# Slot scores and running sum computed transposed, with projections and output products put in another order

## The chip, the core and the metric

One Trainium2 chip, one of its cores. The time is device microseconds for one execution of the whole program, the median of several; lower is better. Engines: PE is TensorE (matmuls), DVE is VectorE, ACT is ScalarE, POOL is GpSimd, SP issues most DMAs. Each runs its own instructions strictly in order and waits on semaphores for the others.

## What is computed

A gated slot attention layer and a scaled linear layer, each followed by a layer norm, for 4 sequences of 512 rows of 512 values, 16 heads. Cut to what matters:

```python
q, k = rope(hs @ Wq.T), rope(hs @ Wk.T); v = hs @ Wv.T; g = hs @ Wg.T
s = clip(hs @ Ws1.T @ Ws2.T + bs2, -32, 32)       # 64 slots for each head
es, enz = exp(s), exp(-cumlogsumexp(s, axis=time))  # enz = 1 / running sum of es
A  = where(mask, q @ k.T * DK ** -0.5, 0)
ok = enz * (A @ es)
qv = softmax(ok)                                   # over the 64 slots
W2 = where(mask, (qv * enz) @ es.T, 0)
o  = W2 @ v
o_n = o * rsqrt(mean(o * o) + EPS) * g_norm_weight
x = layernorm(hs + (o_n * silu(g)) @ Wo.T)
x = layernorm(x + x @ (weight * scale).T + bias)
```

## The kernel before

Four groups of four heads (g), inside each four sequences (b), inside each four chunks of 128 rows (c): 64 steps, written out in line by `all_steps_in_line`. A step i finishes the attention of chunk i and makes the projections, scores and exponentials of chunk n, the next one. Within a sequence two states are carried from chunk to chunk, `s1` (sum of k by es) and `s2` (sum of es by v); chunk 0 begins without them, chunk 3 updates none. Projections and the output product are split in a high and a low part, three products for each of four slices of the contraction: 12 matmuls of 512 columns (L842, called by `project`, or by the output loop into `bank_a`). The others are fp32 matmuls or transposes, which also run on TensorE (`transposes`, L856).

TensorE's order in a step: Q projection of n; `ok` of i (L960 from the masked scores, L962 from the state s1, four heads each, 64 columns wide); transposes of the normed and gated `o_gated` of the chunk before; K projection; transposes of q; slots of n (L982); V projection; transposes of the probabilities `slot_p`; output product of the chunk before into `bank_a`; W2 of i (L1010) and its part from s2 (L1015); transposes of es (n); running sum of es (`running_sum`, L869 to L872); G projection; transposes of k (n); o of i (L1038) out of the masked W2; updates of s1 and s2 (L1044, L1049); scores A of n (L879). A semaphore wait stands ahead of nearly each.

Behind o stands a chain on three engines, called the norm chain here: ScalarE squares o (L600), VectorE gates o (L803), sums the squares (L805) and makes `var` (L808), GpSimd takes `var` to the power -1/2 (L435, `rms`) and multiplies `o_gated` by it (L437). TensorE's transposes of `o_gated` in the next step wait for that. Behind `var` VectorE has in its queue `mask_a` (L673) and, in the step of chunk 0, the low part of the output weights `wo_lo` (L814). When a sequence is the group's last, the steps of chunks 2 and 3 also split the next group's weights: ScalarE makes the high parts (`w_split`, 128x2048), VectorE the low ones (L615); SP loads the next weight once the buffer of one is free.

`ok` is scaled by `enz` and its maximum taken on VectorE (L766, L769), shifted on GpSimd (L444), exponentiated on ScalarE (L567), summed on VectorE (L772) and multiplied by `enz` on GpSimd (L447). VectorE masks W2 at L678, and `enz` is a reciprocal of the running sum (L669).

Names in the trace that are views of others: `batch_raw` holds masked, o_sq, qT, kT, v and gate; `ws_raw` holds ok and slot_p; `small_ops` holds es, s1, s_clip and the constants; `bank_wo` holds W2, o, ok and slots.

Of the kernel before, what the change touches and what calls it, by code (L numbers as in the profile page):

```python
# [21 lines left out]
P = 128  # L22
# [3 lines left out]
HG = 4  # L26
# [20 lines left out]
for name, width in (("cos", CB * 64), ("sin", CB * 128), ("keep", P), ("below", P), ("identity", P), ("gnorm", 1),  # L47
                    ("ws2", HEADS * M)):
    start = sum(stop - first for first, stop in SMALL.values())
    SMALL[name] = (start, start + width)  # L50
# [3 lines left out]
def gated_slot_attention_block(nc, hs_cols, hs_rows, w_groups, ws1, small_in, ffn_w, ffn_scale, ffn_bias, out):  # L54
    with ExitStack() as ctx:
# [6 lines left out]
        def sem(name):  # L62
# [17 lines left out]
        cos_t, sin_t, keep, below_raw, ident, gn, ws2_raw = [small[:, a:b] for a, b in SMALL.values()]  # L80
        keep_r, below_r = sb("keep_r", P, F32R), sb("below_r", P, F32R)
# [10 lines left out]
        ok, slot_p = ws1_raw[:, 0:H], ws1_raw[:, H:2 * H]  # L92
        s1, s_clip, *es = [ws2_raw[:, H * k:H * k + H] for k in range(4)]
# [8 lines left out]
        esT = sb("esT", H)  # L102
        enz = sb("enz", H)
# [4 lines left out]
        pT, s2 = sb("pT", H), sb("s2", H)  # L108
# [5 lines left out]
        bank_qv, bank_kg, bank_t, bank_a, bank_c, bank_s2 = [  # L114
            bank(n) for n in ("bank_qv", "bank_kg", "bank_t", "bank_a", "bank_c", "bank_s2")]
        cums, s1_acc = bank_c[:, 0:H], bank_c[:, H:2 * H]
# [5 lines left out]
        slots_acc = bank_wo[:, H:2 * H]  # L122
        s2_acc = bank_s2[:, 0:H]
# [5 lines left out]
        def o_of(h):  # L129
            start = 512 * (h % 2) + H + P * (h // 2)  # L130
            return bank_wo[:, start:start + P]

# [16 lines left out]
        banks_T, banks_ffn = (bank_c, bank_s2, bank_a, bank_s), (bank_qv, bank_kg, bank_t, bank_o)  # L149
# [3 lines left out]
        for name in ("first", "second"):  # L153
# [15 lines left out]
        a_mm, ok_mm, w2_mm, o_mm, s1_mm, s2_mm, cums_mm = [  # L169
            sem(n) for n in ("a_mm", "ok_mm", "w2_mm", "o_mm", "s1_mm", "s2_mm", "cums_mm")]  # L170
        qT_mm, kT_mm, pT_mm, esT_mm, oT_mm = [sem(n) for n in ("qT_mm", "kT_mm", "pT_mm", "esT_mm", "oT_mm")]
        q_turned, q_summed, k_turned, k_summed = [sem(n) for n in ("q_turned", "q_summed", "k_turned", "k_summed")]
        qT_made, kT_made, v_made, s1_made, s2_made, a_masked, w2_masked = [
            sem(n) for n in ("qT_made", "kT_made", "v_made", "s1_made", "s2_made", "a_masked", "w2_masked")]
        th_made, gate_made, s_clipped, es_made, es_hi_made, es_lo_made, esT_made, enz_made = [
            sem(n) for n in ("th_made", "gate_made", "s_clipped", "es_made", "es_hi_made", "es_lo_made",
                             "esT_made", "enz_made")]
        ok_scaled, ok_maxed, ok_shifted, prob_made, prob_summed, slot_p_made, pT_made = [
            sem(n) for n in ("ok_scaled", "ok_maxed", "ok_shifted", "prob_made", "prob_summed", "slot_p_made",
                             "pT_made")]  # L180
# [203 lines left out]
        def _(pool):  # L384
# [47 lines left out]
            def step(u, g, b, c, last, left):  # L432
# [38 lines left out]
        def _(act):  # L471
# [32 lines left out]

            act.wait_ge(ones_set, 2)
# [6 lines left out]
            copy(keep_r[:, :], keep).then_inc(consts_made, 1)  # L512
            copy(below_r[:, :], below_raw).then_inc(consts_made, 1)
# [15 lines left out]
            from_bank(esT[:, :], bank_t[:, 0:H], esT_mm, 1, esT_made)  # L529
# [28 lines left out]
            def step(u, g, b, c, last, left):  # L558
# [8 lines left out]
                act.activation(ok[:, :], ok[:, :], ACT.Exp).then_inc(prob_made, 1)  # L567
# [45 lines left out]
        def _(dve):  # L613
# [144 lines left out]
            def step(u, g, b, c, last, left):  # L758
# [31 lines left out]
                if not left:  # L790
                    tick(2, 2)
# [343 lines left out]
```

## Time and profile before

| | before |
|---|---|
| median of 3 runs | 1510.54 us (1507.4 to 1511.48) |
| the profiled execution | 1510.89 us, of which 1509.1 us span |
| PE busy | 98% of the span, 9040 instructions |
| DVE busy | 58%, 876.1 us |
| POOL busy | 40%, 599.4 us |
| ACT busy | 35%, 529.3 us |
| mean granted clock of TensorE | 0.997 |
| chain that ended last | PE 96% |

The span runs from the first to the last instruction. The chain that ended last is followed back from the last instruction to whatever released each. A busy share of matmuls includes their pipeline, so what a block of matmuls costs is read here from the start of its first row to the start of the next block's first row.

### The profile page before, as it was taken

Reading aid. Unit: us, or ns where it says so; the run is one execution under the profiler, and the core shown is the slowest. Engines: PE = TensorE matmul, PEld = TensorE weight load, DVE = VectorE, ACT = ScalarE, POOL = GpSimd, SP = SyncE. Lnnn points to the kernel's source line nnn. Section 1 sums busy time; section 2 is a strip of 40 time slices with the busy share of each in tenths; the row PEclk is TensorE's granted clock in tenths of the full one; section 3 lists DMA queues with packets and bytes.
Section 4 is the critical chain, followed back from the end, with each engine's and each line's share of the span. In section 5 each row is a group of like instructions: output and inputs, shape, how many; then the busy total and the mean of one; then the engine's idle time right before and its main releaser. Section 6 shows DMA issues by size and latency. Waiting matters only on the chain.

```text
span 1509.1 us, 22779 instructions
## 1 busy us (share of the span) xinstructions
PE 1481.0 (98%) x9040; PEld 1236.9 (82%) x9040; DVE 876.1 (58%) x1488; ACT 529.3 (35%) x995; POOL 599.4 (40%) x573
## 2 busy tenths in 40 slices
PE   6999999999999999999999999999999999999988
PEld 3788888888888888888888888888888888888866
DVE  4555655556665556556755645555764555556567
ACT  5333323334332323333432323323432322323356
POOL 2424424443442344334434423433542343334345
PEclk9999999999999999999999999999999999999999
DMA  8211112022211202112420211112221111212223
GB/s 297 106 49 36 62 46 74 23 81 100 90 58 46 74 23 74 46 39 79 137 74 23 74 46 39 58 46 95 87 102 46 40 58 46 74 30 74 63 86 123
DMA packets 51414, 106.63 MB, mean 71 GB/s; under 512 B 5360, under 2 KB 15600, under 8 KB 46960
## 3 DMA queue, kind: packets, MB, share of 16 engines
q1 hardware_dynamic: 49008, 101.01, 20.2%
q10 hardware_dynamic: 2304, 4.20, 0.7%
q8 instruction: 72, 1.18, 0.3%
q14 instruction: 30, 0.25, 0.1%
HBM read 82.90 MB, written 22.28 MB: 70 GB/s over the span
## 4 chain that ended last, share of the span: by engine, by line
PE 96%; DVE 2%; DMA 1%; ACT 1%; issue 1%; POOL 0%; SPq 0%; POOLq 0%; DVEq 0%; ACTq 0%
PE bank_kg L842 24%; PE bank_qv L842 24%; PE bank_a L842 12%; PE bank_t L856 8%; PE bank_a L879 5%; PE bank_wo L1038 4%; PE bank_wo L960 3%; PE bank_wo L962 3%; PE bank_wo L1010 3%; PE bank_c L1044 3%; PE bank_s L1049 2%; PE bank_wo L1015 1%; DMA batch_raw<-hs_cols 1%; PE bank_c L869 1%; PE bank_wo L889 1%; PE bank_wo L842 1%
## 5 line engine op out<-in xcount | busy, mean ns | idle before, releaser
L435 POOL TENSOR_TENSOR rms<-var,minus_half 128x4 f32<-128x4 f32 x64 | 65.2, 1019 | 681.5 <-DVE var L808 681.5
L842 PE MATMUL bank_qv<-w_hi,hs_hi 128*128 128x512 f32 x512 | 207.4, 405 | 2.7 <-DVE w_lo L615 2.7
L842 PE MATMUL bank_kg<-w_hi,hs_hi 128*128 128x512 f32 x512 | 207.7, 406 | 1.0 <-DVE rope_b L635 1.0
L842 PE MATMUL bank_kg<-w_hi,hs_lo 128*128 128x512 f32 x512 | 202.3, 395 | 0.0
L842 PE MATMUL bank_qv<-w_hi,hs_lo 128*128 128x512 f32 x512 | 202.0, 395 | 0.0
L842 PE MATMUL bank_qv<-w_lo,hs_hi 128*128 128x512 f32 x512 | 201.8, 394 | 0.0
L842 PE MATMUL bank_kg<-w_lo,hs_hi 128*128 128x512 f32 x512 | 201.8, 394 | 0.0
L789 DVE TENSOR_TENSOR part<-bank_a,part 128x512 f32<-128x512 f32 x64 | 44.2, 691 | 231.8 <-PE bank_a L842 231.8
L473 ACT ACTIVATE oT_hi<-bank_t 128x512 fp32r<-128x512 f32 x65 | 38.9, 599 | 293.2 <-PE bank_t L856 293.2
L401 POOL TENSOR_TENSOR q_rot<-rope_a,rope_b 128x512 f32<-128x512 f32 x64 | 82.3, 1286 | 111.7 <-DVE rope_b L635 111.7
L669 DVE RECIPROCAL enz<-bank_c 128x256 f32<-128x256 f32 x64 | 112.3, 1755 | 9.7 <-PE bank_c L872 3.3
L842 PEld LDWEIGHTS bank_qv<-w_hi,hs_lo 128*128 128x128 f32 x512 | 95.8, 187 | 23.6
L842 PEld LDWEIGHTS bank_kg<-w_hi,hs_lo 128*128 128x128 f32 x512 | 95.8, 187 | 23.5
L842 PEld LDWEIGHTS bank_qv<-w_hi,hs_hi 128*128 128x128 f32 x512 | 96.4, 188 | 21.3 <-issue 3.5
L842 PEld LDWEIGHTS bank_kg<-w_hi,hs_hi 128*128 128x128 f32 x512 | 96.0, 187 | 19.2 <-issue 1.4
L842 PEld LDWEIGHTS bank_kg<-w_lo,hs_hi 128*128 128x128 f32 x512 | 96.2, 188 | 18.0 <-issue 0.2
L842 PEld LDWEIGHTS bank_qv<-w_lo,hs_hi 128*128 128x128 f32 x512 | 96.2, 188 | 17.7
L437 POOL TENSOR_TENSOR o_gated<-o_gated,rms 128x512 f32<-128x512 f32 x64 | 104.2, 1628 | 5.0
L842 PE MATMUL bank_a<-wo_hi,oT_hi 128*128 128x512 f32 x256 | 105.9, 414 | 0.0
L473 ACT ACTIVATE batch_raw<-bank_t 128x512 f32<-128x512 f32 x128 | 76.0, 594 | 78.9 <-PE bank_t L856 78.8
L664 DVE SCALAR_TENSOR_TENSOR batch_raw<-batch_raw,bank_kg 128x512 f32<-128x512 f32 x64 | 43.9, 686 | 101.3 <-ACT batch_raw L590 101.3
L842 PE MATMUL bank_a<-wo_hi,oT_lo 128*128 128x512 f32 x256 | 100.9, 394 | 0.0
(178 smaller groups left out, 3215.6 us busy)
## 6 DMA issues: line engine op xcount, KB each, us to landing
w_raw<-w_groups SPq DMA_DIRECT2D x32, 1024.0 KB, 5.0
x_scratch<-part SPq DMA_DIRECT2D x65, 256.0 KB, 2.0
hs_raw<-hs_cols SPq DMA_DIRECT2D x64, 256.0 KB, 2.8
part<-x_scratch SPq DMA_DIRECT2D x49, 256.0 KB, 2.9
batch_raw<-hs_cols SPq DMA_DIRECT2D x4, 1024.0 KB, 8.2
u_part<-u_scratch SPq DMA_DIRECT2D x64, 64.0 KB, 2.6
part<-hs_rows SPq DMA_DIRECT2D x16, 256.0 KB, 3.2
w_raw<-x_scratch SPq DMA_DIRECT2D x16, 256.0 KB, 2.7
```

What stands on the lines that cost most here:

```text
L401: pool.tensor_tensor(q_rot[:, :], rope_a[:, :], rope_b[:, :], ALU.add).then_inc(q_summed, 1)
L435: pool.tensor_tensor(rms[:, :], var[:, :], minus_half[:, :], ALU.pow).then_inc(rms_made, 1)
L437: pool.tensor_tensor(per_head(o_gated[:, :]), per_head(o_gated[:, :]), over_columns(rms[:, :], DV), ALU.mult).then_inc(o_norm_made, 1)
L473: return act.activation(dst, src, ACT.Copy, scale=scale)
L669: dve.reciprocal(enz[:, :], cums).then_inc(enz_made, 1)
L842: mm = pe.matmul(dst, x, y, start=start and n == 0, stop=stop and n == 2, **kw)
L856: mm = pe.transpose(bank_t[:, P * h:P * h + P], src[:, P * h:P * h + P], ident)
L879: mm = pe.matmul(bank_a[:, P * h:P * h + P], kT[:, P * h:P * h + P], qT[:, P * h:P * h + P], start=True, stop=True)
L960: mm = pe.matmul(dst, masked[:, P * h:P * h + P], es[now][:, slots], start=True, stop=c == 0)
L962: mm = pe.matmul(dst, qT[:, P * h:P * h + P], s1[:, slots], start=False, stop=True)
L1010: mm = pe.matmul(w2_of(h), esT[rows, at], pT[rows, at], start=True, stop=True)
L1038: mm = pe.matmul(o_of(h), masked[:, head], v[now][:, head], start=False, stop=True, skip_group_check=True)
```

## The change

- **`ok` is computed transposed.** es and s1 (64 columns) are now the stationary operand and the masked scores and qT (128 columns) the moving one; two heads go to the upper and lower 64 partitions of the same columns. VectorE scales it with the transposed reciprocal `enzT`, and two transposes on TensorE bring it back (`ok_acc`). VectorE then takes the maximum and does the shift, both from the accumulator; GpSimd's two operations on it are gone.
- **The running sum is fused with the transposes of es.** One product of es_hi/es_lo (stationary) with identity and keep mask side by side gives the transposed es and its transposed sum within the chunk; ScalarE copies both out and adds the last column of the chunk before as a bias. `below` is gone. `pT` is now multiplied by `enzT` on VectorE while it is copied out.
- **Order.** The output product follows the V projection directly. The probabilities' transposes, the fused sum and the G projection come next, then W2. The transposes of k and the updates of s1 and s2 stand ahead of o. s1 and s2 share an accumulator and are copied out by one instruction, ahead of the square of o.

```diff
@@ pool step @@
-                pool.wait_ge(ok_maxed, done(u, c))
-                pool.tensor_tensor(per_head(ok[:, :]), per_head(ok[:, :]), over_columns(ok_max[:, :], M),
-                                   ALU.subtract).then_inc(ok_shifted, 1)
-                pool.wait_ge(prob_made, done(u, c))
-                pool.tensor_tensor(slot_p[:, :], ok[:, :], enz[:, :], ALU.mult).then_inc(slot_p_made, 1)
@@ act @@
+            def turned(slot, n, first):
+                act.wait_ge(sumT_mm, n)
+                copy(two(esT[slot][:, :]), esT_acc).then_inc(esT_made, 1)
+                if first:
+                    copy(two(cumsT[slot][:, :]), cumsT_acc).then_inc(cumsT_made, 2)
+                else:
+                    for r in range(2):
+                        act.activation(cumsT[slot][:, P * r:P * r + P], cumsT_acc[:, r, :], ACT.Identity,
+                                       bias=cumsT[1 - slot][:, P * r + P - 1:P * r + P]).then_inc(cumsT_made, 1)
...
+                if c < CB - 1:
+                    from_bank(states[:, :], bank_c[:, :], states_mm, carried(u, c), states_made)
                 act.wait_ge(o_mm, i)
                 act.activation(by_parity(o_sq[:, :]), paired(1), ACT.Square).then_inc(o_squared, 1)
-                if c < CB - 1:
-                    from_bank(s1[:, :], s1_acc, s1_mm, carried(u, c), s1_made)
-                    from_bank(s2[:, :], s2_acc, s2_mm, carried(u, c), s2_made)
@@ dve step @@
+                dve.wait_ge(okT_mm, i)
+                dve.scalar_tensor_tensor(okT, okT_acc, SCALE, enzT[:, :], ALU.mult, ALU.mult).then_inc(ok_scaled, 1)
+                lo(oT_lo[:, :], bank_t[:, :], oT_hi[:, :], oT_hi_made, i, oT_lo_made)
                 dve.wait_ge(ok_mm, i)
...
+                dve.tensor_reduce(ok_max[:, :], per_head(ok_acc), AX.X, ALU.max).then_inc(ok_maxed, 1)
+                dve.wait_ge(ok_maxed, i)
+                dve.tensor_tensor(per_head(prob), per_head(ok_acc), over_columns(ok_max[:, :], M), ALU.subtract
+                                  ).then_inc(ok_shifted, 1)
                 if left:
                     rotate_k((c + 1) % CB, n)
                     clip(n)
...
+                dve.wait_ge(pT_mm, i)
+                dve.tensor_tensor(pT[:, :], bank_t[:, 0:H], enzT[:, :], ALU.mult).then_inc(pT_made, 1)
+                if left:
+                    dve.wait_ge(pT_made, i)
+                    make_enz((c + 1) % 2, n)
@@ pe @@
+            def turn_and_sum(slot, n):
...
+                for r in range(2):
+                    for x, half in enumerate((es_hi, es_lo)):
+                        mm = pe.matmul(bank_e[:, 2 * P * r:2 * P * r + 2 * P], half[slot][:, P * r:P * r + P],
+                                       ident_keep[:, :], start=x == 0, stop=x == 1)
+                mm.then_inc(sumT_mm, 1)
...
+                    mm = pe.matmul(okT_of(h), es[now][:, M * h:M * h + M], masked[:, head], start=h < 2,
+                                   stop=c == 0, skip_group_check=True)
...
+                        mm = pe.matmul(okT_of(h), s1[:, M * h:M * h + M], qT[:, head], start=False, stop=True,
+                                       skip_group_check=True)
...
+                pe.wait_ge(ok_scaled, i)
+                for r in range(2):
+                    mm = pe.transpose(ok_acc[:, P * r:P * r + P], okT[:, P * r:P * r + P], ident)
+                mm.then_inc(ok_mm, 1)
```

The order on TensorE, from the end of the output product to the first matmul of the G projection. Before:

```order
L842 MATMUL bank_a<-wo_hi,oT_lo 128x512
L1010 MATMUL bank_wo<-pT,esT 128x128 x4
L1015 MATMUL bank_wo<-s,pT 128x128 x4
L856 MATMUL bank_t<-small_ops 128x128 x2
L869 MATMUL bank_c<-es_hi,below_r 128x256
L869 MATMUL bank_c<-es_lo,below_r 128x256
L871 MATMUL bank_c<-es_hi,keep_r 128x256
L872 MATMUL bank_c<-es_lo,keep_r 128x256
L842 MATMUL bank_kg<-w_hi,hs_hi 128x512
```

After:

```order
L864 MATMUL bank_a<-wo_hi,oT_lo 128x512
L878 MATMUL bank_t<-small_ops,ws_raw 128x128 x2
L891 MATMUL bank_e<-ident_keep,es_hi 128x256
L891 MATMUL bank_e<-ident_keep,es_lo 128x256
L891 MATMUL bank_e<-ident_keep,es_hi 128x256
L891 MATMUL bank_e<-ident_keep,es_lo 128x256
L864 MATMUL bank_kg<-w_hi,hs_hi 128x512
```

W2 (L1010, L1015) has left this place, the transposes of es are gone, and those of the probabilities (`ws_raw`) have come from the other side of the output product.

The order on TensorE from the end of the G projection to the Q projection. Before:

```order
L842 MATMUL bank_kg<-w_hi,hs_lo 128x512
L856 MATMUL bank_t<-small_ops,k_rot 128x128 x4
L1038 MATMUL bank_wo<-batch_raw 128x128 x4
L1044 MATMUL bank_c<-small_ops,k_rot 128x64 x4
L1049 MATMUL bank_s<-batch_raw,small_ops 64x128 x4
L879 MATMUL bank_a<-batch_raw 128x128 x4
L842 MATMUL bank_qv<-w_hi,hs_hi 128x512
```

After:

```order
L864 MATMUL bank_kg<-w_hi,hs_lo 128x512
L1046 MATMUL bank_wo<-pT,esT 128x128 x4
L1050 MATMUL bank_wo<-states,pT 128x128 x4
L878 MATMUL bank_t<-small_ops,k_rot 128x128 x4
L1058 MATMUL bank_c<-small_ops,k_rot 128x64 x4
L1063 MATMUL bank_c<-batch_raw,small_ops 64x128 x4
L1073 MATMUL bank_wo<-batch_raw 128x128 x4
L899 MATMUL bank_a<-batch_raw 128x128 x4
L864 MATMUL bank_qv<-w_hi,hs_hi 128x512
```

W2 (now L1046, L1050) stands directly ahead of the transposes of k, and o (now L1073) comes behind the two state updates instead of ahead of them.

TensorE between the Q and the K projection: `ok`, then the transposes of `o_gated`. Before:

```order
L842 MATMUL bank_qv<-w_hi,hs_lo 128x512
L960 MATMUL bank_wo<-small_ops,batch_raw 128x64
L962 MATMUL bank_wo<-small_ops,batch_raw 128x64
L960 MATMUL bank_wo<-small_ops,batch_raw 128x64
L962 MATMUL bank_wo<-small_ops,batch_raw 128x64
L960 MATMUL bank_wo<-small_ops,batch_raw 128x64
L962 MATMUL bank_wo<-small_ops,batch_raw 128x64
L960 MATMUL bank_wo<-small_ops,batch_raw 128x64
L962 MATMUL bank_wo<-small_ops,batch_raw 128x64
L856 MATMUL bank_t<-small_ops,o_gated 128x128 x4
```

After:

```order
L864 MATMUL bank_qv<-w_hi,hs_lo 128x512
L978 MATMUL bank_wo<-batch_raw,small_ops 64x128 x4
L983 MATMUL bank_wo<-batch_raw,states 64x128 x4
L878 MATMUL bank_t<-small_ops,o_gated 128x128 x4
```

The eight alternating products 64 columns wide have become two groups with a 64-column stationary operand.

VectorE from the scaling of `ok` to the sum `eps_sum`, which goes into `var`. Before:

```order
L766 SCALAR_TENSOR_TENSOR ws_raw<-bank_wo,enz 128x256
L769 TENSOR_REDUCE ok_max<-ws_raw 128x4
L615 TENSOR_TENSOR oT_lo<-bank_t,oT_hi 128x512
L772 TENSOR_REDUCE p_sum<-ws_raw 128x4
L629 TENSOR_TENSOR rope_a<-bank_kg,small_ops 128x512
L635 TENSOR_TENSOR rope_b<-bank_kg,small_ops 128x4x64 x2
L659 TENSOR_SCALAR small_ops<-bank_wo 128x256
L778 SCALAR_TENSOR_TENSOR eps_sum<-p_sum 128x4
```

After:

```order
L783 SCALAR_TENSOR_TENSOR ws_raw<-bank_wo,enzT 128x256
L632 TENSOR_TENSOR oT_lo<-bank_t,oT_hi 128x512
L786 TENSOR_REDUCE ok_max<-bank_wo 128x4
L788 TENSOR_TENSOR ws_raw<-bank_wo,ok_max 128x256
L646 TENSOR_TENSOR rope_a<-bank_kg,small_ops 128x512
L652 TENSOR_TENSOR rope_b<-bank_kg,small_ops 128x4x64 x2
L676 TENSOR_SCALAR small_ops<-bank_wo 128x256
L794 TENSOR_REDUCE p_sum<-ws_raw 128x4
L796 SCALAR_TENSOR_TENSOR eps_sum<-p_sum 128x4
```

The maximum and the new shift stand behind the low part of oT, ahead of the rotation of k and the clip; the sum of the probabilities is behind the clip.

## Rows read from the trace of the kernel before

**Rows 1.** The page: the span, and TensorE's busy time and instructions.
```profile
span 1509.1 us, 22779 instructions
PE 1481.0 (98%) x9040; PEld 1236.9 (82%) x9040; DVE 876.1 (58%) x1488; ACT 529.3 (35%) x995; POOL 599.4 (40%) x573
```

**Rows 2.** Timeline of TensorE, 701 to 721 us: start, duration, engine, line, operation, count.
```profile
701.21 1.06 PE L1038 MATMUL bank_wo<-batch_raw 128*128 128x128 f32 x8
702.11 1.00 PE L1044 MATMUL bank_c<-small_ops,k_rot 128*128 128x64 f32 x8
703.04 0.66 PE L1049 MATMUL bank_s<-batch_raw,small_ops 128*64 128x128 f32 x8
703.63 1.16 PE L879 MATMUL bank_a<-batch_raw 128*128 128x128 f32 x8
704.54 0.48 PE L842 MATMUL bank_qv<-w_hi,hs_hi 128*128 128x512 f32 x1
...
707.42 0.33 PE L960 MATMUL bank_wo<-small_ops,batch_raw 128*128 128x64 f32 x2
...
709.15 0.61 PE L856 MATMUL bank_t<-small_ops,o_gated 128*128 128x128 f32 x4
...
712.41 0.60 PE L856 MATMUL bank_t<-small_ops,q_rot 128*128 128x128 f32 x4
...
712.97 0.39 PE L842 MATMUL bank_qv<-w_hi,hs_hi 128*128 128x512 f32 x1
...
715.77 0.38 PE L856 MATMUL bank_t<-small_ops,ws_raw 128*128 128x128 f32 x2
715.91 0.48 PE L842 MATMUL bank_a<-wo_hi,oT_hi 128*128 128x512 f32 x1
...
718.83 0.72 PE L1010 MATMUL bank_wo<-pT,esT 64*128 64x128 f32 x8
...
719.92 0.44 PE L856 MATMUL bank_t<-small_ops 128*128 128x128 f32 x2
720.12 0.36 PE L869 MATMUL bank_c<-es_hi,below_r 128*128 128x256 f32 x1
...
720.67 0.39 PE L842 MATMUL bank_kg<-w_hi,hs_hi 128*128 128x512 f32 x1
```

**Rows 3.** Timeline of GpSimd: the end of a norm chain, chunk 1.
```profile
705.65 1.04 POOL L437 TENSOR_TENSOR o_gated<-o_gated,rms 128x512 f32<-128x512 f32 x1
```

**Rows 4.** Timeline of TensorE, VectorE, GpSimd: the same chain behind chunk 0.
```profile
590.79 1.06 PE L1038 MATMUL bank_wo<-batch_raw 128*128 128x128 f32 x8
...
595.00 2.34 DVE L814 SCALAR_TENSOR_TENSOR wo_lo<-w_raw,small_ops,wo_hi 128x2048 fp32r<-128x2048 f32 x1
...
595.24 3.01 POOL L437 TENSOR_TENSOR o_gated<-o_gated,rms 128x512 f32<-128x512 f32 x1
```

**Rows 5.** Timeline of GpSimd and TensorE: the one time that TensorE waited for it.
```profile
1410.40 2.46 POOL L437 TENSOR_TENSOR o_gated<-o_gated,rms 128x512 f32<-128x512 f32 x1
...
1412.91 0.66 PE L856 MATMUL bank_t<-small_ops,o_gated 128*128 128x128 f32 x4 [0.29 <-POOL o_gated L437]
```

**Rows 6.** Timeline of VectorE: the mask of W2.
```profile
720.04 0.69 DVE L678 TENSOR_TENSOR batch_raw<-bank_wo,small_ops 128x512 f32<-128x512 f32 x1 [0.41 <-PE bank_wo L1015]
```

**Rows 7.** Timeline of VectorE, GpSimd, ScalarE: a step in which weights are split.
```profile
712.61 0.69 DVE L629 TENSOR_TENSOR rope_a<-bank_kg,small_ops 128x512 f32<-128x512 f32 x1 [0.78 <-PE bank_kg L842]
...
715.27 2.28 DVE L615 TENSOR_TENSOR w_lo<-w_raw,w_hi 128x2048 fp32r<-128x2048 f32 x1
...
715.29 2.86 POOL L409 TENSOR_TENSOR es_lo<-small_ops,es_hi 128x256 fp32r<-128x256 f32 x1
...
722.84 1.91 ACT L473 ACTIVATE w_hi<-w_raw 128x2048 fp32r<-128x2048 f32 x1 [2.05 <-DMA w_raw<-w_groups]
```

**Rows 8.** Timeline of GpSimd and VectorE: the end of that step.
```profile
727.86 1.02 POOL L435 TENSOR_TENSOR rms<-var,minus_half 128x4 f32<-128x4 f32 x1 [9.71 <-DVE var L808]
...
728.24 2.28 DVE L615 TENSOR_TENSOR w_lo<-w_raw,w_hi 128x2048 fp32r<-128x2048 f32 x1
```

More of the change, by code:

```diff
@@ L46 @@
 SMALL = {}
-for name, width in (("cos", CB * 64), ("sin", CB * 128), ("keep", P), ("below", P), ("identity", P), ("gnorm", 1),
+for name, width in (("cos", CB * 64), ("sin", CB * 128), ("keep", P), ("identity", P), ("gnorm", 1),
                     ("ws2", HEADS * M)):
@@ L131, in o_of, with okT_of @@
             return bank_wo[:, start:start + P]
+        def okT_of(h):
+            rows, at = slice(64 * (h % 2), 64 * (h % 2) + 64), H + P * (h // 2)
+            return bank_wo[rows, at:at + P]
         def paired(bank_half):
@@ L696, in _ @@
             clip(1)
-            make_enz(1)
+            make_enz(0, 1)
             make_gate(0, 1)
@@ L1002, in step @@
                 mm.then_inc(out_mm, 1)
+                pe.wait_ge(prob_made, i)
+                if left:
+                    pe.wait_ge(qT_made, n)
+                transposes(prob, HG // 2).then_inc(pT_mm, 1)
+                if left:
+                    pe.wait_ge(cumsT_made, 2 * i)
+                    turn_and_sum(nxt, n)
+                    pe.wait_ge(k_turned, n)
+                    if last and c == CB - 1:
+                        w_ready(g * 4 + 8)
+                    project(WG, bank_kg, nxt).then_inc(g_mm, 1)
+                if not left:
+                    tick(1, 1)
                 pe.wait_ge(pT_made, i)
+                pe.wait_ge(esT_made, i)
                 if left:
@@ L1009, in step @@
                     rows, at = slice(64 * (h % 2), 64 * (h % 2) + 64), slice(P * (h // 2), P * (h // 2) + P)
-                    mm = pe.matmul(w2_of(h), esT[rows, at], pT[rows, at], start=True, stop=True)
+                    mm = pe.matmul(w2_of(h), esT[now][rows, at], pT[rows, at], start=True, stop=True)
                 if c:
-                    pe.wait_ge(s2_made, carried(u, c - 1))
                     for h in range(HG):
@@ L1018, in step @@
                 if left:
-                    pe.wait_ge(es_made, n)
-                    transposes(es[nxt], HG // 2).then_inc(esT_mm, 1)
-                    running_sum(nxt, n, c == CB - 1)
-                    pe.wait_ge(k_turned, n)
-                    if last and c == CB - 1:
-                        w_ready(g * 4 + 8)
-                    project(WG, bank_kg, nxt).then_inc(g_mm, 1)
                     pe.wait_ge(k_summed, n)
-                    pe.wait_ge(esT_made, n)
                     transposes(k_rot[nxt]).then_inc(kT_mm, 1)
+                if c < CB - 1:
+                    for h in range(HG):
+                        pe.matmul(s1_acc[:, M * h:M * h + M], k_rot[now][:, P * h:P * h + P],
+                                  es[now][:, M * h:M * h + M], start=c == 0 and h == 0, stop=True,
+                                  skip_group_check=True)
+                    for h in range(HG):
+                        rows, at = slice(64 * (h % 2), 64 * (h % 2) + 64), slice(DV * (h // 2), DV * (h // 2) + DV)
+                        mm = pe.matmul(s2_acc[rows, at], es[now][:, M * h:M * h + M], v[now][:, DV * h:DV * h + DV],
+                                       start=False, stop=True, skip_group_check=True)
+                    mm.then_inc(states_mm, 1)
                 if not left:
-                    tick(1, 1)
                     pe.wait_ge(part_made, i)
@@ L1112 @@
         "keep": keep_mask,
-        "below": 1 - keep_mask,
         "identity": np.eye(P, dtype=np.float32),
```

124 lines of the change are left out of this document (47 added, 77 removed).

## The prediction

> **What bounds the kernel now.** I read the page first: TensorE is busy for 1481.0 of 1509.1 us [rows 1], and the list of waits gives it only a handful in the whole program. So the kernel costs what TensorE's blocks cost, and a change pays by shortening blocks as long as no other engine becomes late. Then the timeline of TensorE over one step: since durations overlap, I take a block from its start to the next one's start [rows 2]. Then, on the timelines of the other engines, what each of TensorE's semaphores would be late by once blocks are shorter or moved. The profiled execution took 1510.89 us, within 0.4 us of the median of the runs (1510.54); the sum is made against 1510.9.
>
> **TensorE's own work.** From [rows 2], per step:
> - `ok` now takes 707.42 to 709.15, 1.73 us for eight products, each 64 columns on a 128-column stationary operand. Afterwards it is eight products with 64 stationary columns, two heads side by side. The update of s2 is that form: four in 703.04 to 703.63, 0.59 us, with going into and out of the half-width layout. The nearest row for eight in one go is W2 with its s2 part, 718.83 to 719.92, 1.09 us, though that halves rows, not columns. The bounds are 0.87 (a pure doubling of the part without the transition, an estimate) and 1.18 (twice 0.59). I take 1.04: 0.69 less. In chunk 0, which has only four: about 0.87 to 0.59, 0.28 less.
> - Two transposes bring `ok` back: +0.21, by the two of es (719.92 to 720.12). The two of es go: -0.20.
> - The output product takes 715.91 to 718.83, 2.92; behind a projection and not behind transposes it costs what V costs, 712.97 to 715.77, 2.80: -0.12. In that 2.92 was 0.04 for the half-array form behind it (Q, which also follows fp32 work, takes 704.54 to 707.42, 2.88); that now falls on G, +0.04, and Q gets another 0.04 for `ok`.
> - The sum keeps four products of 256 columns (720.12 to 720.67, 0.55), but a sequence's first chunk had only two: +0.28 in the step of chunk 3.
>
> Steps of chunks 1 and 2: -0.69 + 0.21 - 0.20 - 0.12 + 0.04 + 0.04 = -0.72 each; chunk 3: -0.44; chunk 0: -0.31. Four make -2.19 us, sixteen sequences -35.0 us. Were that all, the time would be 1476.
>
> **Waits that appear.** Four are ended by rows, and they eat it.
>
> First, the norm chain behind chunk 0. From the start of o at 590.79 GpSimd's multiplication ends at 595.24 + 3.01 = 598.25, 7.46 us later [rows 4]. Behind other chunks it takes 705.65 + 1.04 - 701.21 = 5.48 [rows 2, 3]: GpSimd gets nowhere while VectorE makes `wo_lo`. TensorE used to have s1, s2, the scores, Q and `ok` to do meanwhile, and now s1 and s2 (702.11 to 703.63, 1.52 us) lie ahead of o. It arrives after o 0.90, scores 0.91, Q 2.92 and `ok` 1.04: 5.77 us. In return the mask of A no longer waits for scores that stood behind s1 and s2. It follows `var` directly, and so `wo_lo` starts about 0.4 after the start of `rms`, as the split in [rows 8] does (728.24 against 727.86), and not about 0.86 after it (595.00 against 594.14, which is 595.24 less 1.10) [rows 4]. That brings the chain's end to 6.98, and TensorE started 0.05 behind it the one time it waited (1410.40 + 2.46 to 1412.91) [rows 5]. The wait is 7.03 - 5.77 = 1.26 us, 16 times: 20.2 us. How long `ok` takes doesn't matter here; chain and wait together are fixed.
>
> Second, the same chain behind chunk 3: 5.48 + 0.05 = 5.53 against 0.90 + 0.91 + 2.92 + 0.59 = 5.32, so 0.21, 16 times: 3.4 us. Behind chunks 1 and 2 it is 5.53 against 5.77, no wait, 0.24 of slack.
>
> Third, the mask of W2. It starts 0.12 behind the start of the block after W2 (720.04 against 719.92) and takes 0.69 [rows 2, 6]; with 0.1 for the signal back (an estimate, twice the 0.05 above) o may start 0.91 behind W2's end. G used to cover this. Now the transposes of k do (0.43) and s1 and s2 (1.52); the step of chunk 3 has no updates, and there 0.48 is left, 16 times: 7.7 us. VectorE's other new work ahead of that mask (copy of pT 0.42, reciprocal 1.75 by the groups of the profile) starts with the output product and the fused sum and ends inside G, 2.84 us long; in chunk 0, where ScalarE makes `wo_hi` before it copies the sums, about 0.7 us of cover is left.
>
> Fourth, the group's last sequence. The rotation of k stands behind the maximum and the shift now. It used to start 0.20 behind the transposes of q (712.61 against 712.41). Now it comes after those transposes 0.35, the signal 0.46, the maximum 0.46 and the shift 0.36, 1.63, so 1.43 later [rows 2, 7]. In ordinary steps the fused sum, though it is earlier than the old one by W2, still finds `es_lo` more than a microsecond early. Where VectorE splits weights, GpSimd's `es_lo` is held up by it: 2.86 us long, ending at 718.15, 2.88 behind the start of the split at 715.27 [rows 7]. Shifted by 1.43 it ends 7.17 behind the start of the transposes of q, and the sum is due after 0.35 + 0.21 + 0.20 + 2.80 + 2.80 + 0.14 = 6.50: 0.7 us, in two steps of three sequences. In the first of the two, the high part of the next V weights waits for their load, which waits for that split. It started 5.29 behind the split's end (722.84 against 717.55). Shifted, it ends so late that the copies of kT and the square of o stand behind it: about 0.3 for the scores, and 1.3 for the norm chain, which meets a split as chunk 0's does. Sum 0.7 + 0.7 + 0.3 + 1.3 = 3.0, three times: 9.0 us. The last sequence of all, with the split of the linear layer's weights in the same places, I put at 1.4.
>
> Waits: 20.2 + 3.4 + 7.7 + 9.0 + 1.4 = 41.7. 1510.9 - 35.0 + 41.7 = **1517.6 us**. GpSimd loses 1.35 us of work a step (L444, L447), which pays nothing, as it isn't what is late. VectorE gains about 0.8 us a step at 58% busy. SP's queue is not reordered; its loads of weights come later with the splits, which is in the fourth wait. The new bias copies on ScalarE (two for one, some 0.3 each) end inside G.
>
> **Two rules of the skill.** GpSimd's 3.01 us beside 1.04 and its end 1 us behind VectorE's operation show that one shuts the other out [rows 3, 4]. The Trainium skill, SBUF — State Buffer, section "Who interferes with whom", says that the port pair these engines share goes whole to whichever starts first, a VectorE operation with two SBUF inputs or a GpSimd one that reads SBUF. By that `wo_lo`, once it starts inside `rms`, would itself wait for the end of `rms`. The row speaks against it: the split starts 0.38 into a `rms` and lasts 2.28 [rows 8], no longer than the one that starts just ahead of GpSimd's work [rows 7]. It is a rival below. The Trainium skill, TensorEngine Tiling, section "Key Properties", says that a change of tiling mode drains the engine. The change adds two such changes a step; the 0.04 and the part of 0.59 above are what the rows give for it.
>
> **The rivals.**
> - The covers hold: the mask of W2 and the splits come in time, because VectorE runs a little ahead of my sum. Without the third and the fourth wait it is 1517.6 - 7.7 - 9.0 = 1501, faster. For it: these are sums of half a microsecond built from many terms. Against: W2's mask is one operation behind one block, and short of terms. Chance 0.14. It decides where both vanish; where one of them does, the time is 1508.6 to 1509.9, no difference: 0.25, with a half-width `ok` at its lower bound (32 steps by 0.17, 5 us) among it.
> - The norm chain is not late behind chunk 0 either, and the change pays in full: 1476. That needs GpSimd to multiply beside `wo_lo`, and every chunk 0 shows 3.01 us. Chance 0.04.
> - `rms` shuts out `wo_lo` once they overlap: it starts 0.64 later (1.02 - 0.38), the chain ends so much later behind 16 chunks 0 and three splits: 19 x 0.64 = 12.2, 1530. Chance 0.10.
>
> **How the numbers follow.** The forecast's own case, some 1515 to 1526, has 0.47. About 0.3% (4.5 us) is what a measurement of this kernel can tell from no change. Slower is the forecast and the shut-out, 0.57; same 0.25; faster 0.14 + 0.04 = 0.18. The range from 1501 to 1530 leaves out the full gain and the tails.
>
> **What would show it.** The changed kernel's waits should list TensorE waiting for `o_gated` of GpSimd some 35 times, with about 1.2 us the common long one; for the mask of W2 some 15 times with 0.5; for `es_lo` six times. The `ok` block should take 1.0 to 1.1. A step of chunk 1 should be 0.5 us longer than before, one of chunk 2 0.7 shorter. If the waits for GpSimd are missing, the norm chain was misread; if `ok` takes over 1.2, the tiling was.

## The result

| | before | after |
|---|---|---|
| median of four runs (lowest to highest), us | 1510.18 (1507.4 to 1511.48) | 1524.88 (1523.71 to 1527.88) |
| profiled execution and its span, us | 1510.89, 1509.1 | 1524.71, 1522.9 |

The changed kernel takes 1.0099 times as long, with a 95% interval of 1.0086 to 1.0113: 14.7 us slower. The forecast was 1517.6, slower by 7; the sign and the range held, the size was half of what came. Between the two profiled executions it is 13.8 us.

The page of the changed kernel, its head and the chain that ended last by engine:

```profile
span 1522.9 us, 22779 instructions
...
PE 1459.8 (96%) x9072; PEld 1187.4 (78%) x9072; DVE 895.2 (59%) x1616; ACT 525.0 (34%) x995; POOL 502.5 (33%) x445
...
PE 79%; POOL 8%; DVE 5%; ACT 4%; issue 3%; DMA 1%; POOLq 0%; SPq 0%; DVEq 0%; ACTq 0%
```

TensorE is busy for 21 us less than in [rows 1], and the program is 14 us longer. GpSimd, with 97 us less to do, now holds 8% of the chain that ended last. The list of waits says where (who waited <- for whom: us in total, times, longest):

```profile
PE bank_t L878 <- POOL o_gated L446: 28.3, 36, 1.4
...
PE bank_e L891 <- POOL es_lo L418: 3.8, 6, 0.6
PE bank_wo L1073 <- DVE batch_raw L695: 3.1, 15, 0.2
```

The three kinds of wait that were forecast are all there, and as often as forecast: some 35 for `o_gated`, some 15 for the mask of W2, six for `es_lo`. On TensorE's timeline the 36 for `o_gated` are 16 of 1.24 us behind the chunks 0, 15 of 0.20 behind the chunks 3, three of 1.18 in the last sequences of groups (1.3 forecast) and two of 1.43 and 0.59 in the final sequence. The common long one, behind chunk 0, on the timelines of TensorE, GpSimd and VectorE of the changed kernel (start, duration, engine, line, operation, count; in brackets the idle time before and who ended it), which answers to [rows 4]:

```profile
684.32 1.16 PE L1073 MATMUL bank_wo<-batch_raw 128*128 128x128 f32 x8
685.32 1.06 PE L899 MATMUL bank_a<-batch_raw 128*128 128x128 f32 x8
686.13 0.48 PE L864 MATMUL bank_qv<-w_hi,hs_hi 128*128 128x512 f32 x1
...
689.11 0.66 PE L978 MATMUL bank_wo<-batch_raw,small_ops 128*64 128x128 f32 x8
...
691.44 0.66 PE L878 MATMUL bank_t<-small_ops,o_gated 128*128 128x128 f32 x4 [1.23 <-POOL o_gated L446]
```
```profile
687.77 1.02 POOL L444 TENSOR_TENSOR rms<-var,minus_half 128x4 f32<-128x4 f32 x1 [10.83 <-DVE var L830]
688.87 2.51 POOL L446 TENSOR_TENSOR o_gated<-o_gated,rms 128x512 f32<-128x512 f32 x1
```
```profile
688.15 2.34 DVE L836 SCALAR_TENSOR_TENSOR wo_lo<-w_raw,small_ops,wo_hi 128x2048 fp32r<-128x2048 f32 x1
```

o starts at 684.32, GpSimd ends at 688.87 + 2.51 = 691.38, and TensorE goes on at 691.44. So the chain with its signal takes 7.12 us; 7.03 was forecast. TensorE's own work beside it ends 1.2 us before.

An ordinary step, timeline of TensorE, which answers to [rows 2]; blocks are again taken from start to start:

```profile
704.63 0.71 PE L1046 MATMUL bank_wo<-pT,esT 64*128 64x128 f32 x7
...
705.72 0.66 PE L878 MATMUL bank_t<-small_ops,k_rot 128*128 128x128 f32 x4
706.21 1.00 PE L1058 MATMUL bank_c<-small_ops,k_rot 128*128 128x64 f32 x8
707.14 0.66 PE L1063 MATMUL bank_c<-batch_raw,small_ops 128*64 128x128 f32 x8
707.73 1.16 PE L1073 MATMUL bank_wo<-batch_raw 128*128 128x128 f32 x8
708.73 1.06 PE L899 MATMUL bank_a<-batch_raw 128*128 128x128 f32 x8
709.54 0.48 PE L864 MATMUL bank_qv<-w_hi,hs_hi 128*128 128x512 f32 x1
...
712.52 0.66 PE L978 MATMUL bank_wo<-batch_raw,small_ops 128*64 128x128 f32 x8
713.01 0.61 PE L983 MATMUL bank_wo<-batch_raw,states 128*64 128x128 f32 x8
713.54 0.66 PE L878 MATMUL bank_t<-small_ops,o_gated 128*128 128x128 f32 x4
713.95 0.48 PE L864 MATMUL bank_kg<-w_hi,hs_hi 128*128 128x512 f32 x1
...
716.84 0.60 PE L878 MATMUL bank_t<-small_ops,q_rot 128*128 128x128 f32 x4
717.27 0.38 PE L1004 MATMUL bank_wo<-small_ops,ws_raw 128*128 128x128 f32 x2
717.41 0.37 PE L1008 MATMUL bank_wo<-ws_part,u_part 128*128 128x256 f32 x1
717.61 0.39 PE L864 MATMUL bank_qv<-w_hi,hs_hi 128*128 128x512 f32 x1
```

| block, us | before | forecast | after |
|---|---|---|---|
| Q | 2.88 | 2.92 | 709.54 to 712.52, 2.98 |
| `ok` | 1.73 | 1.04 | 712.52 to 713.54, 1.02 |
| transposes of `o_gated` | 0.37 | 0.37 | 713.54 to 713.95, 0.41 |
| transposes of q, and of `ok` | 0.35 | 0.35 + 0.21 | 716.84 to 717.41, 0.57 |
| output product | 2.92 | 2.80 | 2.74 |
| fused sum, with the transposes of es before | 0.75 | 0.55 | 0.57 |
| G | 2.80 | 2.84 | 2.87 |
| transposes of k | 0.43 | 0.43 | 705.72 to 706.21, 0.49 |
| o and the scores together | 1.81 | 1.81 | 1.00 + 0.81 |

And the steps, from the start of one o to the start of the next (ordinary sequences; a step repeats within 0.02 from sequence to sequence, but for one of 21.07 in the place of 20.95):

| step from the o of chunk | 0 | 1 | 2 | 3 | sequence |
|---|---|---|---|---|---|
| before | 22.69 | 22.69 | 22.46 | 19.89 | 87.7 |
| after | 23.41 | 22.10 | 20.95 | 21.49 | 87.95 |

A sequence is 0.23 us longer, where the forecast had 0.24 shorter: 0.47 x 16 = 7.5 us, and that is the whole miss. The last sequence of each of the first three groups costs 3.1 us on top (forecast 3.0), and the final sequence, taken together with the stretch ahead of the first o, about 0.8 (1.4).

### The profile page after: what moved, and what is told of

Same layout as the page of the kernel before. It is cut to its first block, busy times and chain, and to the rows that moved or that the text cites. A ratio compares the mean times of both kernels' runs of the same rounds, so it can differ in the third digit from the quotient of the medians.

```text
span 1522.9 us, 22779 instructions
## 1 busy us (share of the span) xinstructions
PE 1459.8 (96%) x9072; PEld 1187.4 (78%) x9072; DVE 895.2 (59%) x1616; ACT 525.0 (34%) x995; POOL 502.5 (33%) x445
## 4 chain that ended last, share of the span: by engine, by line
PE 79%; POOL 8%; DVE 5%; ACT 4%; issue 3%; DMA 1%; POOLq 0%; SPq 0%; DVEq 0%; ACTq 0%
PE bank_kg L864 24%; PE bank_qv L864 16%; PE bank_a L864 10%; PE bank_t L878 7%; PE bank_wo L1073 5%; POOL o_gated L446 4%; PE bank_wo L1046 3%; PE bank_c L1058 3%; POOL rms L444 2%; PE bank_e L891 2%; PE bank_c L1063 2%; DVE sum_sq L827 2%; PE bank_a L899 2%; ACT batch_raw L620 2%; PE bank_wo L1050 1%
## 5 line engine op out<-in xcount | busy, mean ns | idle before, releaser
L686 DVE RECIPROCAL enzT<-cumsT 128x256 f32<-128x256 f32 x64 | 112.2, 1753 | 69.5 <-ACT cumsT L521 54.7
L414 POOL TENSOR_TENSOR k_rot<-rope_a,rope_b 128x512 f32<-128x512 f32 x64 | 82.8, 1294 | 209.2 <-DVE rope_b L652 209.2
L825 DVE TENSOR_TENSOR o_gated<-bank_wo,batch_raw 128x512 f32<-128x512 f32 x64 | 44.3, 692 | 126.8 <-ACT batch_raw L620 126.8
L586 ACT ACTIVATE ws_raw<-ws_raw 128x256 f32<-128x256 f32 x64 | 26.9, 420 | 237.8 <-DVE ws_raw L788 237.8
L786 DVE TENSOR_REDUCE ok_max<-bank_wo 128x4 f32<-128x256 f32 x64 | 27.2, 424 | 130.4 <-PE bank_wo L1004 130.4
```

The costliest lines, as they stand in the source:

```text
L414: pool.tensor_tensor(k_rot[slot][:, :], rope_a[:, :], rope_b[:, :], ALU.add).then_inc(k_summed, 1)
L686: dve.reciprocal(enzT[:, :], cumsT[slot][:, :])
L825: dve.tensor_tensor(by_parity(o_gated[:, :]), paired(1), by_parity(gate[c % 2]), ALU.mult).then_inc(o_gated_made, 1)
```

## The experiments

The theory at this point: the cause of the loss is the place of o behind the updates of s1 and s2, which takes 1.5 us of TensorE's work out of the norm chain's cover, while `wo_lo` on VectorE keeps GpSimd's multiplication at 2.5 us. Rivals: W2's new place does it, the new arithmetic does it (its pieces cost more than they save), or `wo_lo` has no part in it. All ratios are against the kernel before on the same chip.

**The new arithmetic in the old order.** W2, the transposes of the probabilities and o stand where they stood; VectorE and ScalarE follow.

```diff
+                transposes(prob, HG // 2).then_inc(pT_mm, 1)
...
                 mm.then_inc(out_mm, 1)
...
-                transposes(prob, HG // 2).then_inc(pT_mm, 1)
...
-                    turn_and_sum(nxt, n)
...
                 mm.then_inc(w2_mm, 1)
...
+                    turn_and_sum(nxt, n)
...
-                    mm.then_inc(states_mm, 1)
...
                 mm.then_inc(o_mm, 1)
...
+                    mm.then_inc(states_mm, 1)
```

> The new arithmetic (ok turned, fused sum) in the old order: probabilities' transposes ahead of the output product, W2 ahead of the fused sum, o ahead of the updates of s1 and s2, the square of o ahead of the copies of the states. Theory (the order lost the gain, by making TensorE arrive at the norm chain's result too early): steps of about 22.2 us behind chunks 1 and 2 as against 22.7 before the change, a wait of 0.2 behind chunk 0, so 1493 us. Rival (the new arithmetic is itself what costs, by its transitions between tilings and its longer way over TensorE and VectorE): 1515 us or more.

Measured: 1499.91 us, 0.9942 (0.9925 to 0.9959), 9.4 us faster than before. Steps are 22.35, 22.16, 22.16 and 19.93. So the arithmetic does pay, and the order costs the changed kernel 25 us. It is 7 us above what I expected. In ordinary sequences the blocks came as computed; the rest lies in the last sequences, and the list of waits names it:

```profile
PE bank_t L877 <- ACT batch_raw L477: 5.3, 6, 0.9
```

The transposes of the probabilities wait there for ScalarE's copy of qT, which stands behind a split of weights.

**Only o ahead again**, ahead of s1 and s2, everything else as changed (the square on ScalarE goes with it).

```diff
-                if c < CB - 1:
-                    for h in range(HG):
-                        pe.matmul(s1_acc[:, M * h:M * h + M], k_rot[now][:, P * h:P * h + P],
...
-                    mm.then_inc(states_mm, 1)
...
                 mm.then_inc(o_mm, 1)
+                if c < CB - 1:
...
+                    mm.then_inc(states_mm, 1)
```

> Of the changed kernel only o goes back ahead of the updates of s1 and s2. Theory: the wait of 1.2 us behind chunk 0 goes, as s1 and s2 (1.5 us) lie behind o again, and in its place o waits some 0.3 us for the mask of W2 in every step, since only the transposes of k lie between: 1510 us. Rival (the norm chain's wait is not what costs): the mask's wait is simply added, 48 x 0.3 on top, 1539 us.

Measured: 1532.38 us, 1.0147 (1.0129 to 1.0166), the slowest version that makes the reference's result, between the two theories' numbers. List of waits, and the o of a chunk 0 and of a chunk 1 on TensorE's timeline:

```profile
PE bank_wo L1063 <- DVE batch_raw L695: 18.7, 63, 0.6
...
PE bank_t L878 <- POOL o_gated L446: 4.6, 19, 0.5
```
```profile
687.68 1.16 PE L1063 MATMUL bank_wo<-batch_raw 128*128 128x128 f32 x8 [0.56 <-DVE batch_raw L695]
...
710.43 1.16 PE L1063 MATMUL bank_wo<-batch_raw 128*128 128x128 f32 x8 [0.21 <-DVE batch_raw L695]
```

The wait for `o_gated` shrinks from 28.3 us to 4.6, but with W2 late and o early the transposes of k alone cover W2's mask, and o waits 63 times. In the step of chunk 0 it is worst: VectorE's reciprocal, which stands ahead of the mask, sat idle for 1.87 us until ScalarE had made `wo_hi` (2.01 us) and copied the sums. My expectation took too little for this wait. In this kernel the two moves go together: with W2 behind G, o is late unless the updates stand ahead of it.

**`wo_lo` out of the chain**: from behind the mask of A in chunk 0 to behind `oT_lo` in chunk 1.

```diff
                 lo(oT_lo[:, :], bank_t[:, :], oT_hi[:, :], oT_hi_made, i, oT_lo_made)
+                if c == 1:
+                    dve.wait_ge(wo_hi_made, u + 1)
+                    dve.scalar_tensor_tensor(wo_lo[:, :], w_raw[0][:, :], gn, wo_hi[:, :].bitcast(F32),
...
-                if c == 0:
-                    dve.wait_ge(wo_hi_made, u + 1)
...
```

> The changed kernel with VectorE's low part of the output weights moved out of the norm chain: from behind the mask of A in the step of chunk 0 to behind the low part of oT in the step of chunk 1, where VectorE is idle. Theory: GpSimd's multiplication takes 1.04 us instead of 3.0 behind chunk 0, the chain is 5.5 us instead of 7.0, the 16 waits of 1.2 us go: 1505 us. Rival (the chain behind chunk 0 is long for another reason, or another wait is right behind it): 1520 us or more.

Measured: 1501.98 us, 0.9957 (0.9942 to 0.9973). One moved operation takes 23 us off the changed kernel. The step from chunk 0 falls from 23.41 to 22.10, 16 x 1.31 = 21.0, and an ordinary sequence takes 86.63 us, as long as in the old order (86.60). Waits, and the group of GpSimd's multiplications (shortest, median, longest in ns):

```profile
PE bank_t L878 <- POOL o_gated L446: 8.7, 21, 1.4
```
```profile
L446 POOL TENSOR_TENSOR o_gated<-o_gated,rms x64: 1038/1039/2458, 40.8 to 1422.9; 128x512 f32<-128x512 f32 x64
```

What is left is 0.20 behind every chunk 3 but the last, 1.17 in the last sequence of each group, and the final sequence. This settles that `wo_lo` beside the chain was needed for the loss. In its new place `wo_lo` starts 0.17 us after another operation of GpSimd, and there it is the one that takes longer, 3.27 us for 2.34 (timelines of VectorE and GpSimd):

```profile
680.14 3.27 DVE L787 SCALAR_TENSOR_TENSOR wo_lo<-w_raw,small_ops,wo_hi 128x2048 fp32r<-128x2048 f32 x1
```
```profile
679.97 1.29 POOL L405 TENSOR_TENSOR hs_lo<-hs_raw,hs_hi 128x512 fp32r<-128x512 f32 x1
```

**Both: old order and `wo_lo` later.** The edits of the first and the third.

```diff
+                if c == 1:
+                    dve.wait_ge(wo_hi_made, u + 1)
...
                 mm.then_inc(o_mm, 1)
+                if c < CB - 1:
...
+                    mm.then_inc(states_mm, 1)
```

> Both at once: the old order with the new arithmetic, and the low part of the output weights in the step of chunk 1. Theory: only 0.2 us behind each chunk 0 is left to gain over the old order alone, 1490 us. Rival: if GpSimd's wait is one of many of equal size, it gains nothing over the old order alone or loses to it, 1493 us or more.

Measured: 1498.15 us, 0.9927 (0.9910 to 0.9944), 11.2 us faster than before: the fastest version of all, though it can't be told apart from the first. The step from chunk 0 stays at 22.39 (22.35 in the first experiment): in the old order the chain had cover enough with `wo_lo` beside it. The span is 2.4 us shorter than the first experiment's (1495.3 for 1497.7), but this is not the moved operation's doing. It lies ahead of the first o, which starts at 61.59 for 63.97 and which the move of `wo_lo` does not reach. TensorE's granted clock from 20 to 40 us was 0.94 there and is 1.00 here. In the final sequence the first step falls from 24.07 to 22.19, yet the third grows from 18.40 to 19.89, at a granted clock of 0.95 instead of 1.00 between 1400 and 1437 us. A difference of 2 us between two single executions can thus be the clock alone.

**Only W2 in its old place**, with the transposes of the probabilities and the reciprocal; o stays behind the updates.

```diff
+                transposes(prob, HG // 2).then_inc(pT_mm, 1)
...
-                transposes(prob, HG // 2).then_inc(pT_mm, 1)
...
-                    turn_and_sum(nxt, n)
...
                 mm.then_inc(w2_mm, 1)
...
+                    turn_and_sum(nxt, n)
```

> Of the changed kernel W2, the probabilities' transposes and the reciprocal go back to their old places; o stays behind the updates of s1 and s2. Theory (each 1.5 us of work taken from behind o costs the norm chain, wherever W2 stands): the waits for GpSimd stay, 1.2 us behind each chunk 0 and 0.2 behind chunk 3; the waits for the mask of W2 (3 us in all) and for es_lo (4 us) go, the transposes ahead of the output product cost 0.06 a step: 1521 us. Rival (it is W2's place that costs): near the old order's 1500 us.

Measured: 1526.29 us, 1.0104 (1.0078 to 1.0130), as slow as the changed kernel. Waits, and the step behind a chunk 0:

```profile
PE bank_t L877 <- POOL o_gated L446: 24.9, 20, 1.5
...
PE bank_t L877 <- ACT batch_raw L477: 5.3, 6, 0.9
```
```profile
690.80 0.66 PE L877 MATMUL bank_t<-small_ops,o_gated 128*128 128x128 f32 x4 [1.24 <-POOL o_gated L446]
```

The mask's 15 waits are gone and the six for qT are back, which I had left out of the number. An ordinary sequence takes 87.73 us, 0.22 less than in the changed kernel, and the steps that end with an o of chunk 3 are 0.31 shorter (20.64 for 20.95). So W2's new place costs little there, and it is not the cause of the loss. The final sequence takes 2.8 us more than in the changed kernel from its first o on; its third step ran at a lower granted clock (0.93 between 1392 and 1462 us).

**`ok` at full width.** The stationary operand of `ok` has 128 columns again, in the changed kernel's order. It computes each pair of heads against both heads' operands, so that `ok` holds mixed sums and isn't the reference's.

```diff
-                    mm = pe.matmul(okT_of(h), es[now][:, M * h:M * h + M], masked[:, head], start=h < 2,
-                                   stop=c == 0, skip_group_check=True)
+                    mm = pe.matmul(bank_wo[:, H + P * (h // 2):H + P * (h // 2) + P], es[now][:, pair],
+                                   masked[:, head], start=h == 0, stop=c == 0, skip_group_check=True)
...
```

> The changed kernel with the stationary operand of ok 128 columns wide, two heads' slots at a time, so that this block stays in the full-array form (its result mixes heads and is not the reference's; the same number of instructions). Theory (the 0.13 us a step that the sum missed is mostly the price of going into and out of the half-width form): from its start to the next block's the Q projection falls from 2.98 to 2.88 us and the transposes of o_gated from 0.41 to 0.37, while ok itself grows from 1.02 to about 1.75. Rival (the projection is longer for what precedes it): Q stays at 2.98. No sum of the whole is staked on it; about 1545 us.

Measured: 1540.13 us in one run. The timeline of TensorE:

```profile
716.20 0.48 PE L864 MATMUL bank_qv<-w_hi,hs_hi 128*128 128x512 f32 x1
...
719.09 1.05 PE L979 MATMUL bank_wo<-batch_raw,small_ops 128*128 128x128 f32 x8
719.98 1.06 PE L985 MATMUL bank_wo<-batch_raw,states 128*128 128x128 f32 x8
720.87 0.60 PE L878 MATMUL bank_t<-small_ops,o_gated 128*128 128x128 f32 x4
721.22 0.48 PE L864 MATMUL bank_kg<-w_hi,hs_hi 128*128 128x512 f32 x1
```
```profile
PE bank_t L878 <- POOL o_gated L446: 9.7, 20, 0.7
```

Q is 2.89 instead of 2.98, `ok` 1.78 instead of 1.02, the transposes behind it 0.35 instead of 0.41. So the half-width form saves 0.76 in itself and costs 0.09 + 0.06 in its neighbours. And the steps from chunk 0 and chunk 3 keep their 23.41 and 21.49 although `ok` is longer in both: there the chain sets the step, and a shorter `ok` only waits longer.

**Old order, `wo_lo` later, and the copy of qT ahead of the weight splits** on ScalarE.

```diff
+                if left:
+                    from_bank(qT[:, :], bank_t[:, :], qT_mm, n, qT_made)
                 if last and c == 2:
                     act.wait_ge(q_mm, n)
                     w_split(WQ, next_raw_in(WQ, g))
...
-                    from_bank(qT[:, :], bank_t[:, :], qT_mm, n, qT_made)
```

> The old order with the new arithmetic and the low part of the output weights in the step of chunk 1, and on ScalarE the copy of qT ahead of the split of the next weights in the steps of chunks 2 and 3 of a group's last sequence. Theory: the six waits of TensorE for that copy (5.3 us in all) go: 1493 us. Rival (something right behind it, such as es_lo, is as late): 1497 us or more.

Measured: 1498.65 us, 0.9927 (0.9901 to 0.9954), nothing gained. The 5.3 us of waits for qT are gone, and others stand right behind:

```profile
PE bank_t L878 <- POOL o_gated L446: 2.9, 4, 1.0
PE bank_wo L1035 <- DVE pT L811: 2.9, 6, 0.5
```

**Control: the kernel before with `wo_lo` later.** The third experiment's edit, made to the kernel before.

```diff
+                if c == 1:
+                    dve.wait_ge(wo_hi_made, u + 1)
...
-                if c == 0:
-                    dve.wait_ge(wo_hi_made, u + 1)
...
```

> Control: the kernel before the change with the same move of the low part of the output weights to the step of chunk 1. Theory: TensorE reached the chain's result 0.48 us after it was there, so only the last sequence can gain: 1508 to 1510 us. Rival (GpSimd's 3 us behind chunk 0 cost something before the change too): 1490 us, as much as in the changed kernel.

Measured, ten runs: 1508.52 us, 0.9995 (0.9984 to 1.0006), no difference; steps stay at 22.69. Only the final sequence changes: its first step falls from 24.13 to 22.69, and its third from 19.52 to 17.96, where the granted clock differs too (0.97 before the edit, 1.00 with it, over the sequence's three steps). GpSimd's multiplications, as above:

```profile
L437 POOL TENSOR_TENSOR o_gated<-o_gated,rms x64: 1040/1042/2820, 43.2 to 1431.1; 128x512 f32<-128x512 f32 x64
```

The collision of `wo_lo` and GpSimd was in the kernel before too, hidden: taking it away there is worth nothing that the ten runs can tell from zero, in the changed order 23 us.

**The kernel before with o behind the updates**, and nothing else of the change (the square on ScalarE goes with it).

```diff
-                pe.wait_ge(w2_masked, i)
-                for h in range(HG):
...
-                mm.then_inc(o_mm, 1)
                 if c < CB - 1:
                     pe.wait_ge(enz_made, n)
...
                     mm.then_inc(s2_mm, 1)
+                pe.wait_ge(w2_masked, i)
+                for h in range(HG):
...
+                mm.then_inc(o_mm, 1)
```

> The kernel before the change with one thing of it alone: o stands behind the updates of s1 and s2, and ScalarE squares o behind the copies of the states. Theory: with the old ok of 1.73 us TensorE arrives 1.00 + 0.82 + 2.88 + 1.73 = 6.43 us after the start of o, and the chain behind chunk 0 takes 7.1, as in the changed kernel: 0.7 us of wait, 16 times, and as much behind the split in three last sequences, 1522 us. Behind chunk 3, where TensorE takes about 5.55 against 5.55, nothing. Rival (moving o is harmless by itself, only the shorter ok makes it late): 1510 us.

Measured: 1531.04 us, 1.0139 (1.0117 to 1.0161). List of waits, and one of them on the timelines of GpSimd and TensorE:

```profile
PE bank_t L856 <- POOL o_gated L437: 10.8, 20, 0.8
```
```profile
600.75 2.52 POOL L437 TENSOR_TENSOR o_gated<-o_gated,rms 128x512 f32<-128x512 f32 x1
...
603.33 0.66 PE L856 MATMUL bank_t<-small_ops,o_gated 128*128 128x128 f32 x4 [0.53 <-POOL o_gated L437]
```

The move alone loses 21 us in the medians; the profiled execution is its fastest, and its span is 16.7 us above [rows 1] (1525.8 for 1509.1). The step from chunk 0 gets 0.74 longer, close to the computed 0.7, which is 12 us. The last sequences of the first three groups cost 1.5 us each on top of that (90.01 for 88.48), where the expectation had 0.7. What the slower executions lost beyond this no trace shows. The wait is 0.5 and not 1.2, since the old `ok` still covers 0.7 of it.

## Why the prediction was right or wrong

**TensorE as the bound, and the counting from start to start**: right. Where nothing waits, steps change by what their blocks change.

**`ok` at half width**: right in itself, 1.02 for 1.04. **The failed step is the price of the neighbours**, a term that was put too small. The prediction put entering the form at "another 0.04" on Q and at the same 0.04 on G. Measured are 0.10 on Q (0.09 of it gone in the experiment at full width) and 0.07 on G. Leaving the form wasn't priced at all: 0.04 to 0.06 on the transposes behind `ok`. The "-0.20" for the transposes of es was too large as well: 0.06 of that was the price of leaving W2's form, which the transposes of k now pay (0.49 for 0.43; with W2 back in its place they take 0.43 again and the fused sum 0.55 + 0.02). This price stood in the rows before the change [rows 2]: behind W2 two transposes took 719.92 to 720.12, 0.20, and behind a projection 715.77 to 715.91, 0.14. Q +0.06, transposes of `o_gated` +0.04, of k +0.06, G +0.03, and 0.02 or less at two more places, less 0.06 on the output product, make some 0.15 a step. The step from chunk 1, where nothing waits, shows 0.13: -0.72 forecast, 22.10 - 22.69 = -0.59 measured. Steps that follow the chain bear only what lies outside it. Over a sequence the 0.47 are 0.18 in the step from chunk 0 (0.09 of it the next point), 0.13 in that from chunk 1, and 0.16 in the other two. The rule of the Trainium skill that the prediction cited, TensorEngine Tiling (Array Packing), "Key Properties", that a change of tiling mode drains the engine, gives no duration. The trace agrees with it in so far as the four changes that can be compared here each have a price, 0.06 to 0.10 us; no row shows a drain as such.

**The norm chain behind chunk 0**: right. 7.12 for 7.03, and the wait 1.23 for 1.26. The 0.09 is o's own block: 1.00 where the scores follow it directly, 0.90 in [rows 2], so its square starts 0.10 later. I had carried the 0.90 over, though the o of a chunk 3 before the change, with its scores directly behind it, took 570.90 to 571.89, 0.99. The step grew by 0.72 where 0.54 was computed, by this 0.09 and by the neighbours above.

**Behind chunk 3**: right, 0.20 for 0.21, and its step follows the chain: 21.49 whether `ok` takes long or not.

**The mask of W2**: right in place, count and size. On the timeline of TensorE in a step of chunk 3 o starts 0.86 behind the start of k's transposes, where 0.91 was forecast; the row shows only 0.20 as idle, since those transposes run for 0.66:

```profile
661.98 0.66 PE L878 MATMUL bank_t<-small_ops,k_rot 128*128 128x128 f32 x4
662.84 1.16 PE L1073 MATMUL bank_wo<-batch_raw 128*128 128x128 f32 x8 [0.20 <-DVE batch_raw L695]
```

**The last sequences**: right, 3.1 for 3.0, and `es_lo` is late six times by what was computed (0.7 from start to start, 0.63 as idle time):

```profile
724.16 0.36 PE L891 MATMUL bank_e<-ident_keep,es_hi 128*128 128x256 f32 x1 [0.63 <-POOL es_lo L418]
```

**The rivals.** That the covers hold (1501) needed the third and the fourth wait to vanish; both are there. The full gain (1476) needed no wait for the chain, and that wait makes 28.3 us in all. The shut-out (1530) falls: `wo_lo` starts at 688.15, 0.38 after the start of `rms`, and takes the 2.34 it took before. The Trainium skill's rule in SBUF — State Buffer, "Who interferes with whom", that whichever starts first keeps the port pair, isn't borne out for this 128x4 operation. For a 128x512 one it is: in the third experiment `wo_lo` starts 0.17 after GpSimd's `hs_lo` and takes 3.27 instead of 2.34. That the total came near this rival's side is due to the neighbours' price, not to its mechanism.

**Cause.** New arithmetic in the old order: 9.4 us faster. The old arithmetic with o behind the updates: 21 slower. That the two add up to 12, near the change's 14.7, is partly luck, for they do not add up step by step. In an ordinary sequence the arithmetic alone saves 1.13 us (86.60 for 87.73) and the move alone costs 0.75 (88.48); together they would save 0.38, and the change costs 0.22. Of these 0.60 the step from chunk 0 holds 0.32: the norm chain sets its length, 23.43 with the old arithmetic and 23.41 with the new, so nothing of the saving is left there. The step that ends with the o of chunk 3 holds 0.31, the cost of W2's new place, since that is what it regains with W2 back. The cause is thus the order: o behind the updates, with `wo_lo` beside the chain, turns a change that is worth 9.4 us into a loss. What stays open is how the waits of the last sequences divide among the three splits: each of the experiments moved them, none took one away alone.

## What to carry to other kernels

Work moved ahead of the start of a long chain is cover taken from that chain: before a block is put ahead of its producer, count from that producer what TensorE still has to do until the result is due, and make the longest case of the chain, not the usual one, the measure. A collision that is hidden (`wo_lo` beside GpSimd's multiplication) is worth nothing until the order changes and then decides it, so it should be moved out of the chain first. A block made shorter between the start of a chain and its late result pays nothing, as `ok` in the steps from the chunks 0 and 3; and a block in another tiling form has to be priced with the block ahead of it and the one behind.

## What the hardware showed that I had not expected

- Entering the half-width form costs about 0.10 us of the 512-column products ahead of it (Q 2.98 against 2.89), leaving it 0.06 of the transposes behind it (0.41 against 0.35), and no row shows idle time for either. It is seen only from start to start.
- Once `wo_lo` runs, GpSimd's multiplication ends about 0.9 us behind it (691.38 against 688.15 + 2.34 = 690.49), and 0.91 in [rows 4] (598.25 against 597.34), where alone it takes 1.04: it gets nearly all of its work done afterwards. The tiny `rms` ahead of it (1.02 for four columns) neither holds `wo_lo` up nor is held up. A GpSimd operation over 128x512 that starts 0.17 ahead of `wo_lo` does hold it up, by 0.93 (3.27 for 2.34), in 15 of the 16 places of the third experiment.
- TensorE's granted clock falls to its lower level, 1.2 GHz, for a few microseconds at places that differ from one execution to the next. In the final sequence of the fourth experiment, behind a wait of 1.60 us, products of 512 columns start 0.43 us apart (from 1424.73 to 1425.16) and soon after 0.23 to 0.24 again (1427.20 to 1427.44).
